# Ten of the output's stores move to GpSimd's queue, in a kernel of a GRU and an expert-choice layer

## What is computed

```python
def cell(h, x):                       # GRU, 256 steps, 16 sequences, 512 columns
    gi = x @ W_ih + b_ih
    gh = h @ W_hh + b_hh
    r = sigmoid(i_r + h_r); z = sigmoid(i_z + h_z)
    n = tanh(i_n + r * h_n)
    return (1 - z) * n + z * h
hs = scan(cell, cond, x)              # 16 x 256 x 512
S = softmax(hs_flat @ router_w + router_b)      # 4096 tokens, 16 experts
G, idx = top_k(S.T, 256)              # each expert takes 256 tokens
y = zeros.at[idx].add(G * (hs_flat[idx] @ expert_w + expert_b))
out = x + y                           # 16 x 256 x 512, float32
```

## Time and profile before

| | us |
|---|---|
| median of 3 runs | 1097.17 (1095.88 to 1097.18) |
| the profiled execution, its own time | 1096.32 |
| its span, from the first to the last instruction | 1094.6 |
| TensorE busy | 1081.6 |
| VectorE busy | 857.2 |
| ScalarE busy | 411.3 |
| GpSimd busy | 15.5 |
| granted TensorE clock, mean | 0.998 |

### The profile page before, as it was taken

How to read it: one execution, slowest core, us unless ns; L and a number is a source line. 1 busy time by engine, 2 the same in 40 slices (tenths; PEclk the granted TensorE clock), 3 DMA queues, 4 the chain that set the end, 5 groups by cost and what they waited for, 6 DMA issues and landing times.

```text
span 1094.6 us, 60966 instructions
## 1 busy us (share of the span) xinstructions
PE 1081.6 (99%) x26752; PEld 892.5 (82%) x26752; DVE 857.2 (78%) x4601; ACT 411.3 (38%) x1658; POOL 15.5 (1%) x42
## 2 busy tenths in 40 slices
PE   7999999999999999999999999999999999999998
PEld 5788888888888888888888888888888888888852
DVE  5788777877777877787777778778788777777897
ACT  1333333434333434333333333333333333333561
POOL 5000000000000000000000000000000000000000
PEclk9999999999999999999999999999999999999999
DMA  7311000000000000000000000000000000000369
GB/s 255 90 22 23 13 13 13 6 11 13 13 13 13 14 13 6 11 13 13 14 13 14 13 5 12 13 13 13 13 13 12 6 12 14 3 3 4 100 175 308
DMA packets 80448, 36.78 MB, mean 34 GB/s; under 512 B 70052, under 2 KB 70308, under 8 KB 80183
## 3 DMA queue, kind: packets, MB, share of 16 engines
q1 hardware_dynamic: 77840, 28.79, 10.8%
q10 hardware_dynamic: 2342, 4.11, 1.2%
HBM read 24.49 MB, written 8.39 MB: 30 GB/s over the span
## 4 chain that ended last, share of the span: by engine, by line
PE 96%; DVE 1%; DMA 1%; SPq 0%; ACT 0%; issue 0%; DVEq 0%
PE gates L819 60%; PE gates L756 26%; PE ffn_ps L883 3%; PE gates L937 3%; DMA whh<-in_L_cond_W_hh 1%; PE gates L915 1%; PE ffn_ps L937 1%; PE log_ps L972 1%; PE gates L949 0%; DVE wih L1417 0%; SPq L376 0%; PE ffn_ps L915 0%; DVE u L1186 0%; SPq L379 0%; DVE wih L1507 0%
## 5 line engine op out<-in xcount | busy, mean ns | idle before, releaser
L819 PE MATMUL gates<-whh,tok 128*16 128x192 f32 x16384 | 713.9, 326 | 3.5 <-DVE tok L1211 1.9
L819 PEld LDWEIGHTS gates<-whh,tok 128*16 128x16 f32 x16384 | 562.5, 123 | 104.5 <-DVE tok L1211 3.3
L518 ACT ACTIVATE th<-gates 128x128 f32<-128x128 f32 x512 | 139.8, 273 | 341.7 <-PE gates L819 341.5
L1186 DVE SCALAR_TENSOR_TENSOR u<-th,gates 128x64 f32<-128x64 f32 x512 | 113.5, 222 | 167.0 <-ACT th L518 166.7
L523 ACT ACTIVATE n_t<-v 128x64 f32<-128x64 f32 x512 | 131.5, 257 | 277.9 <-DVE v L1190 277.9
L756 PE MATMUL gates<-wih,xS 128*32 128x192 f32 x3024 | 146.3, 326 | 0.0
L1202 DVE STREAM_TRANSPOSE nT<-n_t 128x64 f32<-128x64 f32 x512 | 123.7, 242 | 0.0
L1193 DVE STREAM_TRANSPOSE zT<-th 128x64 f32<-128x64 f32 x512 | 122.0, 238 | 0.0
L1190 DVE SCALAR_TENSOR_TENSOR v<-u,gates 128x64 f32<-128x64 f32 x512 | 113.1, 221 | 8.8
L756 PEld LDWEIGHTS gates<-wih,xS 128*32 128x32 f32 x3024 | 100.1, 110 | 21.0
L1211 DVE SCALAR_TENSOR_TENSOR tok<-new_n,z_h 128x32 f32<-128x32 f32 x512 | 110.1, 215 | 8.7
(11 more groups left out here) (202 smaller groups left out, 622.2 us busy)
## 6 DMA issues: line engine op xcount, KB each, us to landing
x_in<-in_x SPq DMA_DIRECT2D x248, 32.0 KB, 2.2
out<-tok SPq DMA_DIRECT2D x15, 256.0 KB, 4.7
xs<-in_x SPq DMA_DIRECT2D x14, 256.0 KB, 3.7
out<-tok ACTq DMA_DIRECT2D x14, 256.0 KB, 4.6
wih<-in_L_cond_W_ih SPq DMA_DIRECT2D x4, 768.0 KB, 7.1
whh<-in_L_cond_W_hh SPq DMA_DIRECT2D x4, 768.0 KB, 13.7
whh<-in_x SPq DMA_DIRECT2D x12, 256.0 KB, 3.6
we<-in_L_ffn_expert_w SPq DMA_DIRECT2D x4, 256.0 KB, 2.8
```

The costliest lines, as they stand in the source:

```text
L518: nc.scalar.activation(th[a][:, :, :].rearrange("p g c -> p (g c)"), gates[t // S % PAIRS][a][:, R_:HN], ACT.Tanh, scale=0.5).then_inc(th_ ...
L819: mm = nc.tensor.matmul(gates[t // S % PAIRS][a][Q * j:Q * j + rows, R_:GC].rearrange("b (g k c) -> b g k c", g=G, k=KH), columns, by_tile ...
L1186: V.scalar_tensor_tensor(u[a][:, :], th[a][:, 0, :], 1.0, ps[a][:, HN:GC], ALU.add, ALU.mult).then_inc(u_ready[a], 1)
```

## The change

Of outputs 0 to 30, SP stores those with i = 0, 3, 6 to 30 (eleven), ScalarE those with i = 1, 4, 7 to 28 (ten), and GpSimd those with i = 2, 5, 8 to 29 (ten), behind its masks, with a semaphore of its own that SP waits for at the end. The two halves of the last tile stay with ScalarE and SP.

```diff
+        stored_by_pool = sem("stored_by_pool")
...
         @block.sync
-            for i in range(0, NT, 2):
+            for i in range(0, NT - 1, 3):
                 sp.wait_ge(out_ready, i + 1)
                 sp.dma_start(out_rows[OUT_ORDER[i]], result(OUT_ORDER[i])).then_inc(stored, 16)
 
             sp.wait_ge(out_ready, NT + 1)
             sp.dma_start(out_rows[NT - 1][:, :, HALVES[1]], xs_tile(NT - 1)[:, HALVES[1]]).then_inc(stored, 16)
-            sp.wait_ge(stored, (NT + 1) * 16)
+            by_pool = len(range(2, NT - 1, 3))
+            sp.wait_ge(stored, (NT + 1 - by_pool) * 16)
+            sp.wait_ge(stored_by_pool, by_pool * 16)
...
         @block.gpsimd
+            for i in range(2, NT - 1, 3):
+                pool.wait_ge(out_ready, i + 1)
+                pool.dma_start(out_rows[OUT_ORDER[i]], result(OUT_ORDER[i])).then_inc(stored_by_pool, 16)
...
         @block.scalar
-                if i % 2:
+                if i == NT - 1:
+
                     act.wait_ge(out_ready, i + 1)
-                    if i < NT - 1:
-                        act.dma_start(out_rows[OUT_ORDER[i]], result(OUT_ORDER[i])).then_inc(stored, 16)
-                    else:
-
-                        act.dma_start(out_rows[i][:, :, HALVES[0]], xs_tile(i)[:, HALVES[0]]).then_inc(stored, 16)
+                    act.dma_start(out_rows[i][:, :, HALVES[0]], xs_tile(i)[:, HALVES[0]]).then_inc(stored, 16)
+                elif i % 3 == 1:
+                    act.wait_ge(out_ready, i + 1)
+                    act.dma_start(out_rows[OUT_ORDER[i]], result(OUT_ORDER[i])).then_inc(stored, 16)
```

## The result

The changed kernel took 1097.77 us (median of 22 runs, 1096.86 to 1099.62) against 1096.16 for the kernel before (22 runs, 1095.05 to 1097.53): a ratio of 1.0016, 95% interval 1.0010 to 1.0022. It is slower, by 1.6 us between the medians and about 1.7 by the ratio. In a second set of runs, on another occasion, the ratio was 1.0016 again (1.0007 to 1.0025). The profiled execution took 1096.86 us, 1.74 around its span of 1095.1, where the kernel before had 1.72: nothing was added outside the span.

A forecast was written before the change was run, and what follows sets the result against it. TensorE, busy 1081.6 of 1094.6 us, was taken as the bound, with its last tile's store and the drain ending nearly together. 0 (issue) + 0 (GpSimd's issue) - 0.2 (drain) gave 1097.0 us, range 1095.9 to 1100.6.

The forecast's parts named there:

- likeliest case: Whole kernel: time the same as before within about 0.2%, 2.2 us; chance 0.78.
- bytes: Last stage's stores: same bytes through 16 full engines; -0.2 us taken of 0 to -0.8, GpSimd's packets 0, +1.5 kept for range.
- Rival C: Last stage: GpSimd's stores hold the DMA engines longer, +1.5 us, 1098.7; chance 0.08.
- -0.2 us of the drain: End of the kernel: last store meets less of its own queue's backlog, -0.2 us of at most 0.8.
- Issue time taken away: Stores' issue in the last stage: 4.0 us off SP and 2.7 off ScalarE, worth nothing to the end.
- Issue time added: GpSimd's store issues, last stage: 1.0 us each, at most 2.6, one per 2.15 us; hidden, so 0.
- Rival B: GpSimd's queue from output 2 on: GpSimd too slow, about 1100.3 us, 1104 at 3.0 us a store; chance 0.17.
- The rule of the Trainium skill: GpSimd's issues beside VectorE's two-SBUF-input pieces: writing descriptors isn't stalled, so the wait is nil.
- the row of the selects: GpSimd's early selects beside VectorE, 1.36 us each: by it an issue may wait a 0.75 us piece, 1.75 in all.
- The last wait: SP's closing wait at the end: near 3 us and on the last tile's store.

The follow-up runs named there:

- gp_all: The kernel before with all outputs 0 to 30 stored by GpSimd, the last tile's halves by ScalarE and SP; ratio 1.0025 (1.0015 to 1.0035).
- gp_early: The kernel before with only outputs 2, 5, 8, 11 and 14 stored by GpSimd, the others alternating as before; ratio 1.0007 (0.9998 to 1.0016).

## Why the prediction was wrong

The forecast was 1097.0 us, 0.2 under the median then shown. The measured 1097.77 lies in the range, and within 0.2% of before as the likeliest case said; the direction was wrong, +1.7 us and not -0.2. That the time came within 0.8 us of the forecast is in part luck: it was reckoned from a median of 1097.17 over three runs, which became 1096.16 over 22.

The step that failed is the one on **bytes**. I read a DMA share of 1.00 to 1.03 as full engines to which a third queue could add nothing, and set the cost of GpSimd's packets to 0 with +1.5 us kept for the range: "No row gives a reason". The term was mis-sized as follows: 0 was put; 0.33 to 0.41 MB more left at the end and a tail longer by 0.9 to 1.5 us were found. Rival C, with 0.08, was the case that came (+1.5 by it, +1.7 measured). Of its mechanism, packets that hold the engines longer, a part was there: for GpSimd's stores 60% of the first stretch per megabyte against 51 to 52% before. It had that for all stores and all the time. The runs show it while the backlog builds up and beside other queues' stores, and not with GpSimd alone (53 to 54%); from 1076 us on it is gone (31.1% for 0.58 MB of GpSimd's against 34.7% for 0.58 of SP's). Why is open, and so is what else late GpSimd stores add to the end (gp_all). A second error of the same step: I wrote that a loss at 1068 us would cost nothing, as the engines are only half busy there. The loss was from 1069 to 1075, where they are all but full, and whatever isn't moved in the first 9 us is carried to the end; gp_early shows it. With that the *-0.2 us of the drain* went too: the three queues left more to drain, not less.

What I had right, by the steps. *Issue time taken away*: worth nothing; ScalarE and SP wait for outputs in both kernels. *Issue time added*: 0.53 us, where I took 1.0 and kept up to 2.6; ten issues keep up with the outputs. The landing times I added to the end of the issue, though they count from its start; this made GpSimd's last store 1.0 us too late and changed nothing. **Rival B**, with 0.17, did not come: GpSimd's issues keep up with the outputs even in gp_all, with one every 0.66 us. The rule of the Trainium skill (SBUF — State Buffer, Who interferes with whom) held, and the row of the selects didn't carry over: beside VectorE's pieces of two SBUF inputs an issue has the same 0.53 us in the middle of them as at 1087.37, and VectorE keeps its 0.74. The 0.4 us by which the prediction let the first byte of GpSimd's path come later were not there: the first data packet came 1.28 us after the start of the first issue on GpSimd (1067.94), and 1.25 us after that on SP (1065.73). *The last wait* is on the last tile's store, as predicted, but the waits for landings are 3.9 us, not near 3.

Of the 1.7 us by the clock, the tail explains 1.16 on the average of two profiles a kernel. The rest is within the scatter of ratios (the kernel before against itself had 0.6 us); whether something ahead of the stage belongs to it stays open.

## What to carry to other kernels

When the DMA engines are full, a further queue has only issue time to save, so look first whether anyone waits for that. Here nobody did, and no kernel with GpSimd stores beat the kernel before. If stores must go to GpSimd's queue as well, an early block of them left no longer tail here, every third one did; that rests on one profile, and the clock doesn't separate the two. And a share of 1.0 isn't a pace: compare GB/s over stages that begin at the same event, since what is lost while a backlog builds up comes back at the end. Count also the bytes that are left when the last producer stops.

## What the runs showed that I had not expected

- Packets of GpSimd's queue have 4096 bytes where the same store by SP or ScalarE has 2048 (640 and 1280 data packets for ten stores).
- SP's and ScalarE's queues shared the engines by packets, not bytes: 602 packets and 1.09 MB against 641 and 0.58 MB in the same 5 us. With GpSimd's queue this was not seen: 179, 316 and 306 packets for 0.58, 0.58 and 0.56 MB.
- An issue on GpSimd (0.53 us, the first one 0.66) was as short as the shortest on SP (0.54) and did not grow with the backlog, where SP's went up to 1.27 us in the kernel before.
- Ten stores in a block by GpSimd were followed by the highest pace of all kernels, 356 GB/s. One profile; not pursued.
- In gp_all the last DMA packet ends 1.3 us before the end of the span, not 0.7 as in the kernel before; SP's closing wait is 0.8 us there, not 0.2. Not pursued.
